# Moving the last-column loads of the expert tiles from GpSimd's queue to SyncE's queue

## What is computed

```python
x = x + 0.5 * _L0_ffn_ref(_layernorm(x), router_w, w1, w2)
x = x + _L0_attn_ref(_layernorm(x), ln_w, ln_b, W_in, conv_w, ...)
x = x + 0.5 * _L0_ffn_ref(_layernorm(x), router_w, w1, w2)
```

```python
logits = jnp.einsum('btd,ed->bte', x, router_w)
top_vals, top_idx = jax.lax.top_k(logits, K)          # K = 2 of E = 8
top_w = jax.nn.softmax(top_vals, axis=-1)
h = jnp.square(jax.nn.relu(jnp.einsum('nd,edh->enh', xf, w1)))   # 256 -> 512
y = jnp.einsum('enh,ehd->end', h, w2)                            # 512 -> 256
out = w_f[0] * y[top_idx[0]] + w_f[1] * y[top_idx[1]]
```

## Time and profile before

| | |
|---|---|
| median of 3 runs | 1157.12 us (1156.86 to 1161.12) |
| profiled execution | 1157.05 us |
| its span in the profile | 1155.0 us, so 2.05 us lie around it |
| mean granted clock of TensorE | 0.951 |
| busy: PE, DVE, ACT, POOL | 946.3, 914.4, 742.8, 589.1 us |
| share of the chain that ended last: PE, DVE | 38%, 33% |
| PE waited for transfers of expert tiles (arena<-disp) | 60.6 us, 6 times |

### The profile page before, as it was taken

One profiled execution on the slowest core, in us unless ns is written; L12 is line 12 of the kernel. 1 busy time (PEld: TensorE's weight loads), 2 busy tenths in 40 slices (PEclk: granted clock), 3 DMA queues, 4 the chain that ended last, 5 costly groups with the idle time before them and its releaser, 6 DMA issues.

```text
span 1155.0 us, 42050 instructions
## 1 busy us (share of the span) xinstructions
PE 946.3 (82%) x14928; PEld 809.8 (70%) x14928; DVE 914.4 (79%) x2840; ACT 742.8 (64%) x1751; POOL 589.1 (51%) x673
## 2 busy tenths in 40 slices
PE   2309998997988999999989899999852699989991
PEld 1209997996966777777777677777631699979990
DVE  6978885663779899999989999999878588645875
ACT  3436655563768888788888788887542376546650
POOL 4853777473644444445434444444357367745551
PEclk9999999998999999999999999999865799989995
DMA  9974565573435656666656665555424366836967
GB/s 270 285 221 89 142 160 144 123 147 84 89 89 107 125 111 116 113 121 125 124 98 118 121 125 115 112 114 96 90 65 129 76 131 144 181 91 142 217 153 236
DMA packets 199018, 154.25 MB, mean 134 GB/s; under 512 B 115808, under 2 KB 165984, under 8 KB 198688
## 3 DMA queue, kind: packets, MB, share of 16 engines
q0 software_dynamic: 43936, 72.96, 30.9%
q1 hardware_dynamic: 146816, 71.23, 26.4%
q10 hardware_dynamic: 8064, 7.38, 2.4%
HBM read 41.37 MB, written 56.10 MB: 84 GB/s over the span
## 4 chain that ended last, share of the span: by engine, by line
PE 38%; DVE 33%; issue 12%; DMA 7%; POOL 4%; ACT 3%; SPq 2%; DVEq 0%; POOLq 0%; ACTq 0%
PE bank L808 16%; PE bank L821 16%; DVE lake L1090 7%; DVE arena L1152 3%; DVE q_ L1070 2%; DVE lake L1097 2%; ACT lake L1377 2%; DMA X<-yg 2%; DMA lake<-turned_y 2%; POOL disp L656 2%; DVE lake L1131 1%; PE bank L1505 1%; PE bank L1574 1%; DVE lake L1119 1%; DMA arena<-disp 1%
## 5 line engine op out<-in xcount | busy, mean ns | idle before, releaser
L808 PE MATMUL bank<-arena,weights 128*128 128x128 f16 x3744 | 242.2, 223 | 63.6 <-DMA arena<-disp 60.6
L808 PEld LDWEIGHTS bank<-arena,weights 128*128 x3744 | 227.7, 100 | 68.9 <-issue 66.0
L755 POOL DMA_INDIRECT ychosen<-arena,didx x156 | 160.6, 1029 | 182.3 <-issue 99.1
L821 PE MATMUL bank<-weights,arena 128*128 x1872 | 232.6, 275 | 2.4 <-DVE arena L929 2.4
L862 ACT ACTIVATE arena<-bank 128x512 f32<-128x512 f32 x156 | 93.2, 598 | 206.1 <-PE bank L808 183.5
L924 DVE TENSOR_TENSOR arena<-arena 128x512 f32<-128x512 f32 x156 | 107.8, 691 | 139.1 <-ACT arena L862 132.0
L821 PEld LDWEIGHTS bank<-weights,arena 128*128 128x128 f16 x1872 | 178.4, 99 | 22.0 <-issue 2.7
L656 POOL DMA_INDIRECT disp<-lake,sloti x128 | 133.2, 1041 | 42.2 <-issue 37.2
L1090 DVE SCALAR_TENSOR_TENSOR lake<-lake,vec 128x128 f32<-128x128 f32 x480 | 128.8, 343 | 0.0
L1239 POOL DMA_DIRECT2D lake<-turned_y x32 | 27.3, 855 | 189.8 <-DMA turned_y<-lake 175.5
L929 DVE TENSOR_TENSOR arena<-arena 128x512 f16<-128x512 f32 x156 | 108.0, 692 | 5.3
(11 more groups left out here) (177 smaller groups left out, 1934.1 us busy)
## 6 DMA issues: line engine op xcount, KB each, us to landing
arena<-in_w SPq DMA_DIRECT2D x16, 512.0 KB, 10.1
yg<-ychosen SPq DMA_DIRECT2D x32, 256.0 KB, 2.8
X<-yg POOLq DMA_DIRECT2D x64, 128.0 KB, 3.6
arena<-lake SPq DMA_DIRECT2D x128, 64.0 KB, 3.3
lake<-lake POOLq DMA_DIRECT2D x32, 256.0 KB, 4.2
turned_y<-lake SPq DMA_DIRECT2D x128, 64.0 KB, 1.8
lake<-turned_y POOLq DMA_DIRECT2D x32, 256.0 KB, 4.2
lake<-ychosen SPq DMA_DIRECT2D x32, 256.0 KB, 3.8
```

The costliest lines, as they stand in the source:

```text
L755: pool.indirect_dma_start(ychosen, bass.IndirectOffsetOnAxis(ap=didx[:, t % NIDX:t % NIDX + 1], axis=0), ysb[n % YB][:, :], None).then_inc ...
L808: mm = pe.matmul(o, chunk(where, 2 * ("hl".index(w) * WN + c * HID + m * P), P), v, start=c == 0 and n_ == 0, stop=c == KD - 1 and n_ == 2)
L821: mm = pe.matmul(down_ps(n), x, chunk(where, 2 * ((2 + "hl".index(w)) * WN + c * D), D), start=c == 0 and n_ == 0, stop=c == KH - 1 and n_ ...
```

## The change

All tails are issued by SP, right behind the transposing load, in all four runs. POOL no longer reads the table of rows, computes addresses or issues tails; its three waits at tile 0 of an odd run, and its waits for `didx` ahead of the tails, go with them. `up` and `take` wait for 32 on `xin_i` everywhere. The scatters of routing between expert tiles and the opening of the state-space block between expert tiles stay where they were.

```diff
-        def pool_tail(q, t):
-            return q % 2 == 1 and t >= XIN
...
         def experts_sync(sp, r, turns=()):
             words = {}
+            def first_row(q, t):
+                if t % THREE == 0:
+                    words[0] = sp.value_load(tabi[q % 2][0:1, t // THREE:t // THREE + 1], min_val=0, max_val=UNITS ** THREE - 1)
...
-                at = first_row(sp, words, q, t)
+                at = first_row(q, t)
...
                 sp.dma_start(xTh[i].rearrange("p (c t) -> p c t", t=P), disp[p][ds(at, P), 0:2 * D], transpose=True)\
                     .then_inc(S(f"xin_{i}"), 16)
-                if not pool_tail(q, t):
-                    sp.dma_start(xtail[i], disp[p][ds(at, P), 2 * D:ROW]).then_inc(S(f"xin_{i}"), 16)
+                sp.dma_start(xtail[i], disp[p][ds(at, P), 2 * D:ROW]).then_inc(S(f"xin_{i}"), 16)
...
         def experts_store(pool, r, routing, turns=()):
             until(routing, ("power", NG - 1))
-            words = {}
...
-                if t + XIN < TILES and pool_tail(q, t + XIN):
-                    if t == 0:
-                        pool.wait_ge(S("table"), q + 1)
-                        pool.wait_ge(S("padded"), 16 * E * (q + 1))
-                        for j in range(HG):
-                            pool.wait_ge(S(f"scat_{j}"), 16 * 2 * GT_ * (q + 1))
-                    at = first_row(pool, words, q, t + XIN)
-                    pool.wait_ge(S("didx"), q * NTAKES + t // NTAKE + 1)
-                    hold(pool, "pool")
-                    pool.dma_start(xtail[t % XIN], disp[q % 2][ds(at, P), 2 * D:ROW])\
-                        .then_inc(S(f"tail_in{t // NTAKE % 2}"), 16)
...
-                pe.wait_ge(S(f"xin_{t % XIN}"), rows_in(q, t))
+                pe.wait_ge(S(f"xin_{t % XIN}"), 32 * (t // XIN + 1 + q * uses(XIN, t % XIN)))
...
-                if pool_tail(q, t0):
-                    dve.wait_ge(S(f"tail_in{t0 // NTAKE % 2}"), tails_in(q, t0))
                 for t in range(t0, t0 + w):
-                    if not pool_tail(q, t):
-                        dve.wait_ge(S(f"xin_{t % XIN}"), rows_in(q, t))
+                    dve.wait_ge(S(f"xin_{t % XIN}"), 32 * (t // XIN + 1 + q * uses(XIN, t % XIN)))
```

More of the change, by code:

```diff
@@ L698, in experts_sync @@
             words = {}
+            def first_row(q, t):
+                if t % THREE == 0:
+                    words[0] = sp.value_load(tabi[q % 2][0:1, t // THREE:t // THREE + 1], min_val=0, max_val=UNITS ** THREE - 1)
+                unit = words[0] >> (UNITS.bit_length() - 1) * (t % THREE)
+                if t % THREE < THREE - 1:
+                    unit = unit & (UNITS - 1)
+                reg = sp.alloc_register(f"row_{q}_{t}")
+                sp.reg_add(reg, sp.to_reg(sp.snap(unit * P)), 0)
+                return sp.snap(reg, donate=True, min_val=0, max_val=E * CAP + (SPARE - 1) * P)
             for s in range(2 * TILES):
```

## The result

The changed kernel takes 1168.3 us in the median of eight runs (1165.0 to 1172.1), the kernel before 1157.6 us in the median of eight runs taken beside them (1155.0 to 1161.1). The ratio is 1.0086, with a 95% interval of 1.0069 to 1.0102: slower by 0.86%, about 10 us. The forecast was 1165.5 us. The profiled execution took 1169.22 us, 12.2 us more than that of before.

A forecast was written before the change was run, and what follows sets the result against it. PE sets the pace while transfers come in time, so how far SP runs ahead of PE decides. The terms 6.4 + 1.5 + 0.5 = 8.4 us on 1157.05 us gave 1165.5 us, range 1158.5 to 1171.

The forecast's parts named there:

- The sign: Whole kernel: the change makes it slower, with a chance of 0.69 (same 0.28, faster 0.03).
- SP's issue time as the resource: Each tail costs SP 0.60 us in its order, and SP's time runs out in q = 3, tiles 18 to 34.
- q = 3, tiles 8 to 18: SP takes 2.51 us a tile instead of 1.92 against PE's 2.65; no PE time is lost, only reserve.
- The lead at tile 18: In q = 3, time from issue of the tile's transposing load to its up: 8.7 us instead of 14.6.
- q = 3, tiles 18 to 34: SP at 3.29 us a tile falls behind PE's 2.65; with 4.9 us of lead needed, PE waits 6.4 us.
- The pattern of waits: In q = 3 from tile 25, PE idles 0.5 to 0.7 us on nearly every tile, some 6 us in sum.
- q = 1, tiles 12 and 13: Tails push the 1 MB load and the transposes behind it later; PE waits 1.5 us, bounds 0 to 3.5.
- q = 1, tile 24: The tail, now issued 1.4 us behind the transpose, moves the end of PE's wait by 0.5 us (0 to 0.7).
- What POOL sheds: 62 tails of about 0.57 us leave POOL; costed at nothing, at most 1.2 us back at two stores in q = 1.
- Hidden after all: Rival: the ring of eight tiles swallows SP's fall-back if SP needs 3.0 us a tile or less; 1157 to 1160, chance 0.16.
- POOL held the chain: Rival: without tails POOL's stores in q = 1 come earlier, shrinking PE's wait before tile 24; 1150 to 1156, chance 0.05.
- DVE becomes the bound: Rival: in q = 3, tiles 18 to 34, late combine loads stop DVE, another 8 us; 1170 to 1176, chance 0.10.

The follow-up runs named there:

- t3: The kernel before with POOL's tails kept, plus a second load of the same 62 tails issued by SP that nobody waits for: 1248.5 us, ratio 1.0110.
- t4: The changed kernel with the 16 combine loads of q = 3 issued by POOL behind tiles 9 to 24 instead of SP: 1237.0 us, ratio 1.0028.
- t8: The changed kernel with q = 3's combine loads on POOL and the 1 MB load moved to behind tile 20 of q = 0: 1159.1 us, ratio 1.0006.
- t6: The changed kernel run once more with no edit: 1169.5 us, ratio 1.0083 against the kernel before.
- t5: The kernel before run once more with no edit: 1158.2 us, ratio 0.9999.
- t2: The kernel before with only the tails of q = 1 moved to SP, those of q = 3 left on POOL: 1236.4 us, ratio 1.0001.
- t9: The edit of t2 repeated on the third chip, only q = 1's tails on SP: 1242.1 us, ratio 1.0006 against the kernel before.
- t7: The changed kernel with the 1 MB load issued behind tile 20 of q = 0 instead of tile 11 of q = 1: 1168.2 us, ratio 1.0073.
- t1: The kernel before with only the tails of q = 3 moved to SP, those of q = 1 left on POOL: 1241.5 us, ratio 1.0059.
- t10: The changed kernel with q = 3's 16 combine loads issued by SP as 8 loads of twice the size: 1248.6 us, ratio 1.0074.
- t12: The kernel before with only SP's fourth yg load moved from behind tile 23 to behind tile 27 of q = 1: 1230.1 us, ratio 0.9920.

## Why the prediction was right

The sign, the place and the mechanism held; two terms were too small, and one error made up for part of another. Predicted was +8.4 us on the profiled execution, it was +12.2 there and +10.8 between the medians, 10 by the ratio.

- **SP's issue time as the resource: right, and shown.** t3 puts only that issue back, and gets the changed kernel's stretches. t4 and t8 take sixteen issues away instead, and the loss of q = 3 shrinks from 9.1 us to 3.0 and 1.9. In time 3.5 us are left in t4, and nothing that can be told in t8 (0.0006), where the early megabyte has its part too. And SP waits for nothing while PE waits for its loads. The rule of the Trainium skill that was set against it, "DMA: Bandwidth & Descriptors", section "Issuing engines are not separate DMA queues", that only sequencer time is saved and is usually small, does not carry here: 0.6 us of sequencer time a tile is small beside a load's landing, but it is a quarter of the 2.65 us that SP has for a tile.
- **q = 3, tiles 8 to 18: the step that was mis-sized.** "The lead at tile 18 becomes 7.29 + 10 × (2.65 − 2.51) = 8.7": it was 4.81 (6.05 in t6). Of the 3.9 us, 1.7 were missing at tile 8 already (5.56). SP took 2.56 us a tile up to there, and PE came sooner: in before PE restarted q = 3 at half clock and took 1.3 us longer for the first two tiles, which had counted as lead: t5, the same kernel with a restart at full clock, has 6.30 us at tile 8 and not 7.29. The other 2.2 us are SP's cost of a tile, 2.73 (t6 the same) and not 2.51. Most of that is not in the issues: they take 1.86 us of a tile against 1.77 in the first eight tiles of before, and what lies between them takes 0.87 against 0.75, with four loads of a table word in ten tiles where the eight tiles had two. Long issues (2.75 at 1059.75, 2.16 at 1068.58; six of the 26 transposes of tiles 8 to 33 took over 1.4 us) are in both averages, and in the trace of before too, so the average over eight tiles did hold them. So the reserve was not reduced, it was gone.
- **q = 3, tiles 18 to 34: direction right, price 0.12 too high.** Predicted 3.29 us a tile, measured 3.17 (t6 3.23). The combine load takes SP 0.43 us in the median when it stands behind a tail, where it took 0.58 behind a transpose, so the tail adds less here than 0.60. The needed lead was put at 4.9 us and was 5.67 at tile 34. With measured values the prediction's formula gives 16 × (3.17 − 2.65) − 4.81 + 5.67 = 9.2 us, which is PE's loss by the definition of the lead, and shows where the 2.8 us over the predicted 6.4 come from: 3.9 from the lead at tile 18 and 0.8 from the lead needed, less 1.9 for a rate that was too high. The last took part of the error off by luck; with a lead of 8.7 the measured rate would have cost 5.3 us.
- **The pattern of waits: partly right.** Predicted were pieces of 0.5 to 0.7 us on nearly every tile from tile 25. There were nine pieces of 0.4 to 1.5 us between tiles 20 and 34, and they sum to 7.4 us. They come in lumps.
- **q = 1, tiles 12 and 13: place right, too small.** Predicted 1.5 us, in bounds of 0 to 3.5. Against PE's wish for tile 12 the transpose was issued 0.8 us later than predicted (232.12, with PE wanting the tile at 236.83; predicted 230.6 and 236.12), and it was there 0.5 us later behind its issue. The wait was 2.61 us, and the slow clock of tile 12's down added 1.3 us, a cost that the prediction did not have: up of 11 to up of 13 took 9.4 us and not 5.3, of which about 1 us came back later. In t2 and t9 the wait came without the slow clock, in t3 with it. In t7, without the megabyte, the wait went and two others came, in t8 one small one.
- **q = 1, tile 24: too high.** Predicted +0.5; the wait went from 6.67 to 6.28 us. The tail landed 2.09 us after its issue, and PE started 3.93 us behind the transpose's issue (277.44 to 281.37), sooner than the 4.68 of the earlier trace rows.
- **What q = 1 costs in time: open.** Traces give 1 to 4 us (t2 +4.3 against t1, t6 +4.2 against t5, t9 0.8 to 1.6). The times of t2 and t9 give 0.1 and 0.7 us by the ratios, 1.8 and −0.7 by the medians, and each is known to about 3 us only.
- **What POOL sheds: nothing, as costed, where the prediction looked.** POOL's accumulation did not come earlier: SP's transpose behind the second wait starts 20.26 us after up of tile 18 (277.44 − 257.18), before it was 20.24 (272.26 − 252.02). In t3, with POOL's tails kept, q = 1 and q = 3 are no longer than under the change; its time is, by 3 us or by nothing, as said there.

The rivals. *Hidden after all* is out by the interval (1.0069 at least). Its condition was SP at 3.0 us a tile or less, and the change has 3.17; t10, with 3.01, still lost 7.6 us in q = 3, since the reserve it relied on is not there. *POOL held the chain* is out by the 20.26 us. *DVE becomes the bound* has its condition fulfilled and not its price: DVE did stop for the combine loads, 13.2 us in eleven pieces, but in that stretch PE is named as waiting for transfers alone, and these waits, with the 0.17 us that each hides, make 8.9 of the 9.2 us. No run took DVE's waits away by themselves, so a small part could be theirs.

## What to carry to other kernels

An engine that only issues transfers has a budget too: count its issues between two steps of the engine it feeds, each at its own duration, add all that lies between them (registers, table loads), and compare the sum with the pace of the consumer. A tail of 1.5 KB moved to it cost some 0.6 us of its time here, and what it used up first was the lead; so price the lead at the place where the queue is fullest, from more than one trace, and beware of a lead that was only there because the consumer had been slow. To tell a feeder that is out of time from loads that land late, ask whether the feeder waits for anything. And before moving the work of a queue, look at what the queue waits for in order: placing one waiting load four tiles later was worth 9.9 us, as much as this change cost.

## What the runs showed of the hardware

- Chips differ more than the two kernels do. Before took 1158.1 us on one chip and 1234.6 and 1242.7 on two others. Most of the difference is in the runs that scatter between expert tiles: q = 0 takes 140 to 145 us there (109 to 111 on the first), q = 2 139 to 147 (109 to 110). q = 1 and q = 3 are the same to a microsecond where nothing in them was changed (t1 and t2 against before). Busy time from 83 to 196 us, which is mostly q = 0, in t5:

```profile
83.00:196.00 113.00, 107.24 (x1511) 101.57 (x1511) 84.69 (x267) 68.44 (x131) 68.98 (x67) 1.00 0.57 134
```

  And the same stretch in t12, on one of the two others:

```profile
83.00:196.00 113.00, 90.81 (x1144) 81.76 (x1145) 69.94 (x237) 49.33 (x98) 46.31 (x46) 0.95 0.43 97
```

  POOL issues 46 instead of 67 instructions in the same time, and 97 instead of 134 GB/s move. What makes it so wasn't tried.
- SP's issues of one kind are not all alike: 1.20 us for most transposes, and about every 10 us one of 1.5 to 2.8 us. In the changed kernel's q = 3 long issues at 1045.5, 1059.8, 1068.6, 1081.0, 1090.2 and 1100.4 us each come within 0.8 us of a packet of the queue that the page calls q8, instruction (1045.1, 1060.5, 1069.4, 1081.3, 1089.7, 1100.8), and before has the same pattern. It is no strict one: a long issue at 1093.9 has no packet of q8 so near, and a packet at 1110.3 no long issue. That instruction loading causes them is a reading of these times and was not tested. The Trainium skill, "Runtime: NRT & Kernel Launch", section "Instruction fetch mechanics", says that the fetch of the next instructions is mostly hidden; if this reading is right, it is not hidden on SP, and where SP's time is the bound each one costs 0.5 to 1.5 us of it.
- A pause of 2.61 us in PE was followed by half clock over tile 12's down. The stretches before that down, over it and behind it (the third number from the end is the granted clock):

```profile
236.00:239.60 3.60, 1.00 (x10) 0.65 (x7) 1.39 (x2) 2.10 (x5) 0.52 (x1) 1.00 1.22 194
241.06:243.60 2.54, 2.54 (x14) 1.82 (x13) 1.38 (x2) 1.23 (x2) 0.00 (x0) 0.50 0.44 104
243.70:249.00 5.30, 5.30 (x71) 5.06 (x70) 2.20 (x7) 3.64 (x8) 2.02 (x3) 0.95 0.51 79
```

  It isn't the length of the pause alone. Ahead of tile 0 of q = 3 PE stood for 3.7 to 4.3 us in the six traces of the faster runs (before, after, t5 to t8). In the profiled execution of before, up and down of that tile then took 2.74 and 2.77 us:

```profile
1020.53 2.74 PE L808 MATMUL bank<-arena,weights 128*128 128x128 f16 x24 [3.80 <-DMA arena<-disp]
1023.06 2.77 PE L821 MATMUL bank<-weights,arena 128*128 x12
```

  In that of the changed kernel they took 1.51 and 1.47, at full clock, though the idle time was nearly the same:

```profile
1024.46 1.51 PE L779 MATMUL bank<-arena,weights 128*128 128x128 f16 x24 [3.73 <-DMA arena<-disp]
1025.80 1.47 PE L792 MATMUL bank<-weights,arena 128*128 x12
```

  t5, the same kernel as before, restarted at full clock too (up in 1.51 us after 3.87 us idle), and t6, the same as the changed one, did not (up in 2.27 and down in 2.41 us after 4.26 us idle). So this 1.3 us on tiles 0 to 2 belongs to no edit.
